# A six-attention decoder stack on one core: row maxima in 32-row array tiles, two at a time, and a new hand-written order

## The reference, cut to what matters

```python
s = einsum('bhqd,bhkd->bhqk', q, k) * scale   # six times, 16 heads
# attention 0: keys within 64 tokens behind the query, and a slope per head
# attention 2: keys up to the query;  attentions 1, 3, 4, 5: all 512 keys
a = softmax(s, axis=-1)
o = einsum('bhqk,bhkd->bhqd', a, v)
x = layernorm(x + o @ wo + bo)
```

## Time and profile before

| | |
|---|---|
| time, median of 3 runs | 4043.79 us (4033.54 to 4052.99) |
| the profiled execution: its own time, its span | 4040.29 us, 4038.5 us |
| mean granted TensorE clock | 0.986 |
| PE busy | 3822.6 us (95%) |
| PE weight load busy | 2101.7 us (52%) |
| DVE busy | 2467.9 us (61%) |
| ACT busy | 2118.9 us (52%) |
| POOL busy | 1142.7 us (28%) |

### The profile page before, as it was taken

How to read it: one execution, slowest core, us unless ns; L and a number is a source line. 1 busy time by engine, 2 the same in 40 slices (tenths; PEclk the granted TensorE clock), 3 DMA queues, 4 the chain that set the end, 5 groups by cost and what they waited for, 6 DMA issues and landing times.

```text
span 4038.5 us, 61075 instructions
## 1 busy us (share of the span) xinstructions
PE 3822.6 (95%) x22860; PEld 2101.7 (52%) x23156; DVE 2467.9 (61%) x5623; ACT 2118.9 (52%) x2727; POOL 1142.7 (28%) x1051
## 2 busy tenths in 40 slices
PE   5999999999989999999989999999998999999998
PEld 3645645555555554555455455544545456555453
DVE  2575576655666477665566547666565755766556
ACT  0465465555545456555644555555554554554555
POOL 2422232222432232222242223222224322322223
PEclk8999999999999999999999999999999999999999
DMA  5211221122221131121222122112132212112111
GB/s 203 89 61 48 78 86 48 58 63 87 70 81 48 48 116 48 48 69 53 87 91 67 43 78 84 48 48 73 57 96 86 75 51 81 61 45 68 48 47 51
DMA packets 259270, 281.29 MB, mean 70 GB/s; under 512 B 24978, under 2 KB 251154, under 8 KB 255378
## 3 DMA queue, kind: packets, MB, share of 16 engines
q1 hardware_dynamic: 258980, 277.37, 21.3%
HBM read 196.79 MB, written 79.69 MB: 68 GB/s over the span
## 4 chain that ended last, share of the span: by engine, by line
PE 85%; DVE 7%; ACT 3%; SPq 2%; issue 1%; DMA 1%; POOL 1%; another core or an unknown queue 0%; DVEq 0%; POOLq 0%; ACTq 0%
PE pv L673 14%; PE st L648 13%; PE mx L722 12%; PE mx L613 12%; PE mx L590 8%; PE st L700 8%; DVE row_max L870 4%; PE mx L725 4%; PE st L599 4%; PE st L738 2%; PE mx L682 2%; ACT probs L785 2%; SPq L496 2%; PE st L627 1%; PE st L689 1%
## 5 line engine op out<-in xcount | busy, mean ns | idle before, releaser
L870 DVE TENSOR_REDUCE row_max<-mx 128x1 bf16<-128x512 f32 (+4 forms) x3072 | 1706.1, 597 | 748.5 <-PE mx L613 388.9
L785 ACT ACTIVATE probs<-st 128x1024 f32<-128x1024 f32 (+1 forms) x1344 | 1261.3, 977 | 738.5 <-PE st L648 463.7
L946 POOL TENSOR_TENSOR qm<-q_high,own_rows 128x512 bf16<-128x512 bf16 x768 | 792.6, 1041 | 1847.6 <-PE mx L613 949.0
L613 PE MATMUL mx<-k_high,qm 128*128 128x512 bf16 (+4 forms) x2776 | 849.3, 345 | 52.1 <-DVE row_max L870 44.5
L648 PE MATMUL st<-q_packed,k_packed 97*128 97x512 bf16 (+2 forms) x3072 | 825.2, 348 | 57.2 <-DMA q_packed<-max_rows 24.6
L673 PE MATMUL pv<-probs,va 128*32 128x512 f32 (+2 forms) x6144 | 707.5, 533 | 7.5 <-ACT probs L785 2.2
L613 PEld LDWEIGHTS mx<-k_high,qm 128*128 128x128 bf16 x3072 | 290.5, 98 | 615.3 <-DVE row_max L870 280.7
L648 PEld LDWEIGHTS st<-q_packed,k_packed 97*128 97x128 bf16 (+1 forms) x3072 | 286.7, 99 | 353.1 <-issue 73.0
L891 DVE TENSOR_TENSOR y<-mx,row 128x256 f32<-128x256 f32 x288 | 121.9, 424 | 430.5 <-PE mx L725 430.3
L722 PE MATMUL mx<-w2s,hid 128*128 128x256 f32 x1536 | 348.4, 380 | 0.4
L700 PE MATMUL st<-xT,w1s 128*128 128x512 f32 x768 | 344.2, 592 | 0.4
(11 more groups left out here) (93 smaller groups left out, 3672.3 us busy)
## 6 DMA issues: line engine op xcount, KB each, us to landing
k_packed<-k_parts_dram SPq DMA_DIRECT2D x576, 128.0 KB, 2.7
q_packed<-q_parts_dram SPq DMA_DIRECT2D x576, 128.0 KB, 2.7
q_parts_dram<-q_low SPq DMA_DIRECT2D x96, 256.0 KB, 2.1
k_parts_dram<-k_low SPq DMA_DIRECT2D x96, 256.0 KB, 2.1
w1s<-w_dram SPq DMA_DIRECT2D x12, 1024.0 KB, 5.1
w2s<-w_dram SPq DMA_DIRECT2D x12, 1024.0 KB, 7.2
q_parts_dram<-q_high SPq DMA_DIRECT2D x48, 256.0 KB, 2.1
k_parts_dram<-k_high SPq DMA_DIRECT2D x48, 256.0 KB, 2.1
```

The costliest lines, as they stand in the source:

```text
L613: mm = pe.matmul(bank[:, 0:k1 - k0], qm[:, h % RING, i * P:(i + 1) * P], high["k"][s][:, t, k0:k1], start=True, stop=(k_kind == FULL))
L785: act.activation(dst[:, :, 0:w], held["scores", b, a, n, e][:, :, 0:w], ACT.Exp, scale=ATT_SCALE[a]) \
L870: dve.tensor_reduce(row_max[s][:, i, h:h + 1], held["max", b, a, h, i][:, 0:k1 - k0], AX_X, ALU.max, negate=True).then_inc(*mx_drained.mar ...
L946: pool.tensor_tensor(qm[:, h % RING], high["q"][s][:, h // HT], own_rows[:, h % HT:h % HT + 1].to_broadcast([P, TOK]), ALU.mult) \
```

## The change

**Maxima two at a time.** A group is no longer four neighbouring heads but every other head of eight (`heads_of`): 0, 2, 4, 6, then 1, 3, 5, 7, and the same of the upper eight. One mask then keeps the 16 rows of four heads at once, one in each 32 rows, so there are four masks a loop. The maximum's matmul takes 32 rows of masked queries and keys in place of 128; a stage issues two of them, for heads j and j + 1 of a group, one after the other, each with a bank and a signal of its own. Hiding and slopes are still added by matmuls over 128 rows, after both.

**The row's DMA.** ScalarE issues it, right behind its own copy.

**Statistics.** BN_AGGR per 128-token block, then one addition of epsilon for both; the seven small operations go.

**The order.** All MERGE strings are new; stages of maxima are half as many (1536). A wait is added for DVE ahead of a projection's rest, for POOL's low part of the loop before.

```diff
+DUO = 2
+AHEAD = GRP + DUO
+def heads_of(g):
+    return slice(g // KT * HT + g % KT, (g // KT + 1) * HT, KT)
...
@@ maxima_stages
-    for h in heads:
-        if h and h + RING - 1 < H:
-            yield "mask", b, a, h + RING - 1
+    for first in firsts:
         for i in range(TT):
-            yield "max", b, a, h, i
+            yield "max", b, a, first // GRP, first % GRP, i
@@ sync, "max_rows"
-                    sp.wait_ge(*st_drained.past(("row", b, a, g)))
-                    sp.dma_start(packed["q"][MAXROW:MAXROW + 1, g * GRP:(g + 1) * GRP], max_rows[:, g % 2]) \
-                        .then_inc(max_row_in[g], 16)
@@ tensor, "max"
-                    bank = held["max", b, a, h, i] = mx_bank()
-                    mm = pe.matmul(bank[:, 0:k1 - k0], qm[:, h % RING, i * P:(i + 1) * P], high["k"][s][:, t, k0:k1],
-                                   start=True, stop=(k_kind == FULL))
...
+                    for j in range(first, first + DUO):
+                        rows_of = slice(j * PAIR, (j + 1) * PAIR)
+                        bank = held["max", b, a, g, j, i] = mx_bank()
+                        mm = pe.matmul(bank[:, 0:k1 - k0], qm[rows_of, g, i * P:(i + 1) * P],
+                                       high["k"][s][rows_of, t, k0:k1], start=True, stop=(k_kind == FULL))
+                        if k_kind == FULL:
+                            mm.then_inc(*max_filled.mark(("max", b, a, g, j, i)))
+                    for j in range(first, first + DUO):
+                        bank = held["max", b, a, g, j, i]
+                        if k_kind == CAUSAL:
+                            mm = pe.matmul(bank[:, i * P:k1], tb("eye"), tb("hide_qk"), start=False, stop=True)
...
@@ scalar, "max_rows"
+                    act.wait_ge(*st_drained.past(("row", b, a, g)))
+                    act.dma_start(packed["q"][MAXROW:MAXROW + 1, heads_of(g)], max_rows[:, g % 2]) \
+                        .then_inc(max_row_in[g], 16)
@@ vector, "project"
+                    if LOOP_NO[b, a]:
+                        dve.wait_ge(*pool_step.past(("l", *before(b, a), m)))
@@ vector, "stats"
-                    dve.tensor_tensor(sm1[:, 0, at], e, odd, ALU.add)
...
-                    dve.tensor_scalar(sm1[:, 6, at], sm1[:, 5, at], 1.0 / D, EPS, ALU.mult, ALU.add) \
+                    for i in (2 * half, 2 * half + 1):
+                        ins = dve.bn_aggr(moments[:, i, :], st6[:, i, :])
+                    chain(ins, ("moments", b, tag, half))
+                    dve.tensor_scalar(spread_of[:, at], moments[:, at, 1], EPS, None, ALU.add) \
@@ gpsimd, "mask"
-                    pool.tensor_tensor(qm[:, h % RING], high["q"][s][:, h // HT],
-                                       own_rows[:, h % HT:h % HT + 1].to_broadcast([P, TOK]), ALU.mult) \
+                    pool.tensor_tensor(qm[:, g], high["q"][s][:, g // KT],
+                                       own_rows[:, g % KT:g % KT + 1].to_broadcast([P, TOK]), ALU.mult) \
@@ MERGE
-    "11": "000211011001121211010211120002122000022120202111010101112111211112121111110212212222002000202111"
-           "00100101101012121222222222220020220220222022022202020020022222022200022020000",
+    "11": "001022100102001221222020021001000100102210210021212211021002222022120210210010010100212222222222"
+           "002020020020020020200002202020200",
```

## The result

The changed kernel takes **3940.32 us** (median of 4 runs, 3937.46 to 3941.93), against 4047.56 us for the kernel before in the same comparison: ratio 0.9739, interval 0.9713 to 0.9766. That is 107 us between the medians and 105 us by the ratio, taken on the 4040 us of the profiled execution. The sign and the order of magnitude were right; 41 us were not foreseen.

What follows compares the result with a forecast made beforehand. PE's feed was taken as the bound, with some 0.3 ms of waits. From 4040 us: -232 overlap, +196 changes of form, -38 row's DMA, +10 ACT's issues, giving 3976 us; range 3880 to 4075.

Steps and rivals of the forecast that it cites:

- PE's feed as the bound: Whole kernel before: feeding PE takes about 3.53 ms, with changes of form 3.69 of 4.04 ms; some 0.3 ms is waits.
- the price of a change of form: PE switching between full array, narrow columns and 32-row pairs: 0.093 us each, 2113 more of them, +196 us.
- Side by side: Maxima's matmuls: the second of each pair overlaps the first, starting 28 ns later; -232 us (-265 to -186).
- rival D: Maxima's matmuls: pairs don't run side by side at all, so the -232 us goes; 4208 us, chance 0.06.
- Rival B: Maxima's matmuls: the second of a pair starts 58 ns later, nothing else changes; +46, 4022 us, chance 0.15.
- The row's DMA: Starts of the last three pairs of batches: ScalarE's issue removes PE's stalls and the low clock behind them; -38 us.
- ScalarE's cost: ACT's queue: 192 issues and waits for its own copy delay the exponentials behind them; +10 us (0 to +60).
- the rest, priced at nothing: Merged statistics (105 us less DVE time), masks leaving POOL, DVE's new wait and the heads' stride: no effect on the time.
- other PE stages cover this chain: Norm's statistics on DVE: other PE work hides them, so 105 us less DVE time gains nothing.
- rival A: PE: leaving the 32-row form costs 0.05 us, or the new order gives back a third of waits; 3900 us, chance 0.17.
- Rival C: PSUM banks: a pair's second matmul waits for DVE; at 0.1 us a pair +154, 4130 us, chance 0.15.
- The sign that I had given for C: PE's waits for row_max: 100 us more of them would show that pairs wait for a bank.

Runs made afterwards that it cites:

- experiment 2: The changed kernel, same order and groups of heads, with each maximum's matmul over all 128 rows and one mask per head (16 a loop): 3966.43 us.
- experiment 3: The changed kernel with one part undone, SyncE issuing the maxima's row again in place of ScalarE: 3952.93 us.
- experiment 1: Kernel before with ScalarE issuing the row: 4020.16 us; merged statistics added: 3997.87 us. Changed kernel with the seven old statistics operations: 3963.13 us.
- experiment 4: The changed kernel with the MERGE strings of before, each stage of two maxima where the second of the two old ones stood: 4222.55 us.

## Why the prediction was right, and where it was short

**Right.** *PE's feed as the bound* and *the price of a change of form*: 0.09 read between full array and narrow columns held for the 32-row form, 0.095 in and 0.10 out. The count, 3885, is exactly what the trace has. *Side by side*: rival D is dead; 1287 of 1536 second matmuls start within 10 ns, most of them at 3 or 4. I took 28, so that term was 232 forecast and 269 if nothing else delayed them. The Trainium skill (TensorE: Matmul & The Clock Gate, Measured speedup vs the span model) has the tiles' starts about 4 ns apart, and this trace agrees with 3 to 4. But 249 of them came later, 117 by over 0.2 us, and all lateness adds up to 74 us: the term measured **-201 us**, within 31 of the forecast. That nearness is luck: I had priced 28 ns of start for every pair and nothing for waits, and the trace has 3 ns for most and long waits for a few, 48 ns in the mean. Rival B is dead with it. *The two terms cancel*: forecast -36 together, and -201 + 201 (2113 x 0.095) by the traces, about nothing, where each second matmul of the comparison follows without a wait. Against the real one, experiment 2, the pairs and their four masks give 30 us.

*The row's DMA*: -38 + 10 = -28 forecast, -23 measured alone in the old order and -15 in the new. The stall was read rightly and vanished; the clock share was mis-sized, as the 1070 to 1156 stretch shows. ScalarE's cost, priced at 10 us, left no mark on the wait in which I had looked for it (104.0 us against 103.1, experiment 3).

**Short.** The step that failed is "**the rest, priced at nothing**", and in it the sentence on the statistics, "other PE stages cover this chain". The statistics gave 25 us alone and 23 in the new order, a fifth of the 118 us they shrank by. A reading that fits is that DVE, though busy for only 60%, paces the banks in some stretches and has no time to spare there; the traces show this only in part (the later second matmuls of experiment 1). The other missing piece is the order: I put it into rival A ("gives back waits") and nothing into the sum; with single maxima it gave 27 us, most of which can be clock. My sum had 15 us of clock, all under the row's stalls. Step by step from the kernel before, forecast and measured: the row's DMA 28 and 23 us, the statistics 0 and 25, the order 0 and 27, the pairs with their masks 36 and 30. That is 64 and 105, and the difference is the 41 us. Rival A was half right, by its second half; a change out of the 32-row form is not cheaper.

**Rival C** was argued against by the spacing of the new strings, and that was the right reason: in the order of before the pairs do wait, and it costs 225 us and not the 154 priced. The number missing in its price was the clock. The Trainium skill (TensorEngine Tiling, PSUM Bottleneck) says that tiling makes TensorE faster but not the emptying of PSUM, and the traces agree: DVE's reduction takes 687 ns as before (688), and in both of the other orders tried the side-by-side form loses. The sign that I had given for C, PE waiting 100 us more for row_max, came up although C is wrong: the weight loads' wait went from 280.7 to 445.5 us, the matmuls' fell from 44.5 to 21.9. It was a poor sign, since a weight load mostly waits while an earlier matmul still streams.

## What to carry to other kernels

Before laying matmuls over one another in array tiles, count the changes of form: here each costs about 0.1 us, so one pair of 512 columns on its own among full-array work earns 17 ns, and narrower ones lose. Tiles need banks free at the same moment, so the spacing of their stages (one latency plus one reduction) decided over the sign here, and an order tuned for single matmuls has to be redone. And of a bundle of edits, the small ones can be worth as much as the one in the title: here merged statistics gave 23 to 25 us, the pairs with their masks 30. Compare the granted clocks as well as the times: most of what the new order gained here can be clock.

## What was not expected of the hardware

TensorE fell to the half clock without one long stall: in experiment 4 it was fed one 0.21 us matmul each 0.60 us from 203 to 205 us and then waited 1.41 us, and from 204 to 216 us the granted clock was 0.73, 0.50 and 0.50, with the work dense again from 211.5 on. Short waits for DVE cost PE twice here.

And a change of form costs the same, 0.09 to 0.10 us, between full array and narrow columns, full array and 32 rows, or 32 rows and narrow columns (1499.00 to 1499.32 in the first timeline above): what is small in a form does not make it cheaper to leave.
